# GpSimd waits for the end of its long instructions and adds the variance's epsilon in the attention half of a two-layer kernel

## The chip, the cores and the metric

One Trainium2 chip, one of its cores. A core has TensorE (PE, matrix products), VectorE (DVE), ScalarE (ACT), GpSimd (POOL) and SyncE (SP), which issues the DMAs here. Each engine runs its own instructions in order, and the engines meet at semaphores only. The metric is the device time of one execution in microseconds (us).

## The reference

Eight sequences of 1024 tokens with 256 channels go through attention in linear form (softmax over the 16 channels of a head for q, softmax over the tokens for k), a layer norm, an output projection, a residual and layer norm, and then a ternary feed-forward layer with its own residual and norm. The part around the change, all in f32:

```python
q = jax.nn.softmax(q, axis=-1)
k = jax.nn.softmax(k, axis=-2)
state = jnp.einsum('bhnd,bhne->bhde', k, v)
out = jnp.einsum('bhnd,bhde->bhne', q, state)
mu = out.mean(-1, keepdims=True)
var = out.var(-1, keepdims=True)
out = (out - mu) * jax.lax.rsqrt(var + EPS) * ln_g + ln_b
return out @ Wo.T + bo
...
x = _layernorm(x + attention(x))
```

## The kernel before

The program has two halves. The attention half takes the first 330 us, the feed-forward half the rest; the change touches the first only. Operands of the products are split into a rounded high part and the rest (`xt_hi`, `xt_lo`), and each product is made of three matmuls (high by high, low by high, high by low).

The attention half is a software pipeline. A loop of ten passes (b from 0 to 9) runs on every engine, and in pass b an engine does pieces of several sequences: the k product, the transposes and the state sum of sequence b, the q product and q denominator of sequence b+1, and the attention product, residual and norm of sequences b-1 and b-2. The order of the pieces within a pass is written out by hand for each engine. A sequence is eight token tiles of 128; g is 0 or 1 and names a group of four.

GpSimd's pass: `norm_rstd` of sequence b-2 (seven small instructions for each g), `q_normalise` twice (L299), `tok_lo` (L280, `xt_lo`), `q_denominator` of g=0 (L335, L337, L340, L343), `tok_lo`, `chan_lo` (L271, `xc_lo`), `tok_c` twice (L290, adds a row to the residual input), `attention_rstd` of g=0 (L308, `rsA` = `veA` to the power -1/2), `chan_lo`, `attention_rstd` of g=1, `q_denominator` of g=1. The instructions at L271, L280, L290 and L299 work on 1024 elements of each partition and have no wait of their own between them, except where an input comes from another engine.

VectorE's pass has, in the part that matters: `product_stats` (L684, `bnA`, the statistics of a tile of the attention product in PSUM `aps`), after tile 4 `out_variance` of g=0 (four aggregations L662 and then L664, `veA` = variance + EPS, for which GpSimd's L308 waits), then `product_stats` of tile 5 and the following, `out_variance` of g=1, `et_low`, then `residual` of g=0 (four instructions at L673, which read `z` and `xt`, and L678, `znm`), `sum_low` (L510, `xe_lo`), and `residual` of g=1.

ScalarE copies each tile of `aps` out (L411) after its statistics; TensorE may write the tile after next only then (L940). At the end of a pass TensorE finishes the state sum (L957), makes the first part of the next k product (L882), and then waits for `xe_lo` to make the state product (L896). After this come the q product and the transposes of the state (L907), ScalarE's `st_hi` (L417), its normalisation of the older sequence and, last, `xt_hi` (L380), which releases GpSimd's first `tok_lo` (L280) of the next pass. SyncE loads a sequence's `xt` and `xc` and stores the result ahead of need.

Of the kernel before, what the change touches and what calls it, by code (L numbers as in the profile page):

```python
# [27 lines left out]
ALU = mybir.AluOpType  # L28
# [4 lines left out]
EPS = 1e-5  # L33
# [14 lines left out]
def wait_for(eng, semaphore, count):  # L48

    if not isinstance(count, int) or count > 0:  # L50
        eng.wait_ge(semaphore, count)
# [24 lines left out]
def attention_phase(nc, kept, x_tok, x_chan, wq, wk, wv, wo, w1, w2, vecs_d, rows_d, ident_d, mask_d, x1_scratch):  # L76

    NB, _, T, C = x_tok.shape
    N = T * P
    CH = C // P  # L80
# [3 lines left out]
    GROUP = 4  # L84
    NG = T // GROUP
# [5 lines left out]
    with ExitStack() as ctx:  # L91
        def sb(name, shape, dt=F32):
            return ctx.enter_context(nc.sbuf_tensor(name, shape, dt))

        def sem(name):
            return ctx.enter_context(nc.semaphore(name))
# [48 lines left out]
        mvA = sb("mvA", [P, T, 2])  # L145
        veA = sb("veA", [P, T])
# [7 lines left out]
        eps = sb("eps", [P, T])  # L154
# [22 lines left out]
        xc_hi_ok, xc_lo_ok = sem("xc_hi_ok"), sem("xc_lo_ok")  # L177
        xt_hi_ok, xt_lo_ok, xt_c_ok = sem("xt_hi_ok"), sem("xt_lo_ok"), sem("xt_c_ok")
        k_mm, k_max, k_maxb, k_bias, k_exp = (sem(s) for s in ("k_mm", "k_max", "k_maxb", "k_bias", "k_exp"))
        q_mm, q_max, q_sub, q_exp = (sem(s) for s in ("q_mm", "q_max", "q_sub", "q_exp"))  # L180
        q_sum, q_inv, q_norm = (sem(s) for s in ("q_sum", "q_inv", "q_norm"))
# [7 lines left out]
        ap_mm, a_stat, a_var, a_eps, a_rstd = (sem(s) for s in ("ap_mm", "a_stat", "a_var", "a_eps", "a_rstd"))  # L189
# [72 lines left out]
        @block.gpsimd  # L262
        def _(pool):
            nc.gpsimd.memset(nhalf[:], -0.5).then_inc(half_ok, 1)

            def chan_lo(b, c):
                if not 1 <= b < NB:
                    return
                pool.wait_ge(xc_hi_ok, b + 1)
                wait_for(pool, k_mm, CH * (b - 1))  # L270
                nc.gpsimd.tensor_tensor(xc_lo[:, b % 2, c], xc[:, c], xc_hi[:, b % 2, c].bitcast(F32), ALU.subtract  # L271
                                        ).then_inc(xc_lo_ok, 1)

            def tok_lo(b, g):
                if not 0 <= b < NB:
                    return
                ts = slice(g * GROUP, (g + 1) * GROUP)
                pool.wait_ge(xt_hi_ok, b + 1)
                wait_for(pool, xe_mm, b)
                nc.gpsimd.tensor_tensor(xt_lo[:, ts], xt[:, b % 2, ts], xt_hi[:, ts].bitcast(F32), ALU.subtract  # L280
                                        ).then_inc(xt_lo_ok, 1)

            def tok_c(b, g):
                if not 0 <= b < NB:
                    return
                ts = slice(g * GROUP, (g + 1) * GROUP)
                pool.wait_ge(xt_lo_ok, NG * b + g + 1)
                if b == 0:
                    pool.wait_ge(rows_ok, 2)
                nc.gpsimd.tensor_tensor(xt[:, b % 2, ts], xt[:, b % 2, ts],  # L290
                                        c_row[:].rearrange("p (o c) -> p o c", o=1).to_broadcast([P, GROUP, C]),
                                        ALU.add).then_inc(xt_c_ok, 1)

            def q_normalise(b, g):
                if not 0 <= b < NB:
                    return
                pool.wait_ge(q_inv, NG * b + g + 1)
                v = qw[:, b % 2, g * GROUP:(g + 1) * GROUP].rearrange("p t (h d) -> p (t h) d", d=D)
                nc.gpsimd.tensor_tensor(  # L299
                    v, v, qinv[:, g].rearrange("p (h o) -> p h o", o=1).to_broadcast([P, GROUP * HEADS, D]),  # L300
                    ALU.mult).then_inc(q_norm, 1)

            def attention_rstd(b, g):
                if not 0 <= b < NB:
                    return
                gs = slice(g * GROUP, (g + 1) * GROUP)
                pool.wait_ge(a_eps, NG * b + g + 1)
                nc.gpsimd.tensor_tensor(rsA[:, gs], veA[:, gs], nhalf[:, gs], ALU.pow).then_inc(a_rstd, 1)  # L308

            def norm_rstd(b, g):  # L310
                if not 0 <= b < NB:
                    return
                gs = slice(g * GROUP, (g + 1) * GROUP)
                n = NG * b + g + 1
                pool.wait_ge(z_sq, T * b + GROUP * (g + 1))
                nc.gpsimd.tensor_tensor(vaZ[:, gs], zss[:, gs], inv_c[:, gs], ALU.mult).then_inc(z_var, 1)
                pool.wait_ge(z_var, n)
                nc.gpsimd.tensor_tensor(veZ[:, gs], vaZ[:, gs], eps[:, gs], ALU.add).then_inc(z_eps, 1)
                pool.wait_ge(z_eps, n)
                nc.gpsimd.tensor_tensor(rsZ[:, gs], veZ[:, gs], nhalf[:, gs], ALU.pow).then_inc(z_rstd, 1)  # L320
                pool.wait_ge(z_rstd, n)
                nc.gpsimd.tensor_tensor(nmr[:, gs], znm[:, gs], rsZ[:, gs], ALU.mult).then_inc(z_fin, 1)
                nc.gpsimd.tensor_tensor(vaZ[:, gs], vaZ[:, gs], rsZ[:, gs], ALU.mult).then_inc(z_fin, 1)
                pool.wait_ge(z_fin, 4 * n - 2)
                nc.gpsimd.tensor_tensor(vaZ[:, gs], vaZ[:, gs], rsZ[:, gs], ALU.mult).then_inc(z_fin, 1)
                pool.wait_ge(z_fin, 4 * n - 1)
                nc.gpsimd.tensor_tensor(z[:, gs, C], vaZ[:, gs], eps[:, gs], ALU.add).then_inc(z_fin, 1)

            def q_denominator(b, g):
                if not 1 <= b < NB:  # L330
                    return
                n = NG * (b - 1) + g
                pool.wait_ge(q_exp, NG * b + g + 1)
                v = qw[:, b % 2, g * GROUP:(g + 1) * GROUP].rearrange("p t (h d) -> p (t h) d", d=D)
                nc.gpsimd.tensor_tensor(qtree[:, g], v[:, :, 0:8], v[:, :, 8:16], ALU.add).then_inc(q_tree, 1)  # L335
                pool.wait_ge(q_tree, 3 * n + 1)
                nc.gpsimd.tensor_tensor(qtree[:, g, :, 0:4], qtree[:, g, :, 0:4], qtree[:, g, :, 4:8], ALU.add  # L337
                                        ).then_inc(q_tree, 1)
                pool.wait_ge(q_tree, 3 * n + 2)
                nc.gpsimd.tensor_tensor(qtree[:, g, :, 0:2], qtree[:, g, :, 0:2], qtree[:, g, :, 2:4], ALU.add  # L340
                                        ).then_inc(q_tree, 1)
                pool.wait_ge(q_tree, 3 * n + 3)
                nc.gpsimd.tensor_tensor(qsum[:, g], qtree[:, g, :, 0], qtree[:, g, :, 1], ALU.add).then_inc(q_sum, 1)  # L343

            nc.gpsimd.memset(inv_c[:], 1.0 / C).then_inc(half_ok, 1)
            nc.gpsimd.memset(eps[:], EPS).then_inc(half_ok, 1)
            pool.wait_ge(half_ok, 3)
            for c in range(CH):
                chan_lo(1, c)
            for b in range(NB + 2):  # L350
                norm_rstd(b - 2, 0)
                norm_rstd(b - 2, 1)
                q_normalise(b, 0)
                q_normalise(b, 1)
                tok_lo(b, 0)
                q_denominator(b + 1, 0)
                tok_lo(b, 1)
                chan_lo(b + 2, 0)
                tok_c(b, 0)
                tok_c(b, 1)  # L360
                attention_rstd(b - 1, 0)
                chan_lo(b + 2, 1)
                attention_rstd(b - 1, 1)
                q_denominator(b + 1, 1)
# [140 lines left out]
        def _(dve):  # L505
# [148 lines left out]
            def out_variance(b, g):  # L654
                if not 0 <= b < NB:
                    return
                ts = range(g * GROUP, (g + 1) * GROUP)
                gs = slice(g * GROUP, (g + 1) * GROUP)
                dve.wait_ge(a_stat, T * b + GROUP * (g + 1))
                nc.vector.memset(fence[:], 0.0)  # L660
                for t in ts:
                    nc.vector.bn_aggr(mvA[:, t], bnA[:, t]).then_inc(a_var, 1)  # L662
                dve.wait_ge(a_var, T * b + GROUP * (g + 1))
                nc.vector.tensor_scalar(veA[:, gs], mvA[:, gs, 1], EPS, None, ALU.add).then_inc(a_eps, 1)  # L664

            def residual(b, g):
                if not 0 <= b < NB:
# [78 lines left out]
            for b in range(NB + 2):  # L746
# [29 lines left out]
                pt_low(b, 0)  # L776
                product_stats(b - 1, 4)
                out_variance(b - 1, 0)
                product_stats(b - 1, 5)
                pt_low(b, 1)  # L780
# [816 lines left out]
```

## Time and profile before

| | us |
|---|---|
| median of 3 runs (637.6 to 639.22) | 637.66 |
| the profiled execution, its own time | 639.02 |
| span of the profile | 637.2 |
| attention half, about | 0 to 330 |
| GpSimd's first `tok_lo` of passes 1 to 6, starts | 70.1, 105.4, 143.7, 178.3, 214.5, 249.8 |

The profile shows for every instruction its start, its length and, where its engine was idle before it, which instruction of which engine released it. An engine name with nothing else is its work; "idle before" is the time in which it had none. Lines are those of the kernel before. Passes 1 to 5 are alike but for some preparation of the feed-forward weights on VectorE and ScalarE at the ends of passes 1 to 4.

### The profile page before, as it was taken

To read this page: it belongs to the slowest core of one execution; us is meant where nothing else is said; L and a number is where in the kernel's file an instruction comes from. 1 tells how busy PE (TensorE), PEld (TensorE's weight loads), DVE (VectorE), ACT (ScalarE), POOL (GpSimd) and SP (SyncE) were. 2 spreads that over 40 slices of the span, in tenths; PEclk is the share of its full clock that TensorE was granted. 3 is DMA by queue.
4 is the path that set the end of the run, shared out by engine and by line. 5 is a ranking of instruction groups with operands and counts; after the bars stand their busy time and mean duration, and the time that the engine had idled before them with its cause. 6 is when DMAs were issued, how large, how long until landed. Compare 5 with 4: busy or idle time off the path is not lost. (4 is left out here: it accounts for less than half of the span.)

```text
span 637.2 us, 10896 instructions
## 1 busy us (share of the span) xinstructions
PE 559.3 (88%) x3584; PEld 505.6 (79%) x3584; DVE 527.3 (83%) x1309; ACT 463.6 (73%) x906; POOL 427.5 (67%) x414
## 2 busy tenths in 40 slices
PE   1879999889998989979652999999999999999991
PEld 1769989879988979968551799888888888888890
DVE  3895798997979897868443479999999999999985
ACT  1253668476865848575554788999999999999983
POOL 0277887969988887783341556766767666776661
PEclk9899999989999999989685799999999999999996
DMA  7411004070402203030105100211112222200002
GB/s 269 168 67 67 1 6 194 1 264 2 163 36 91 109 2 133 1 132 2 66 8 225 33 34 2 62 55 53 53 46 67 68 67 67 68 34 33 34 34 99
DMA packets 10712, 46.53 MB, mean 73 GB/s; under 512 B 1312, under 2 KB 1568, under 8 KB 8352
## 3 DMA queue, kind: packets, MB, share of 16 engines
q1 hardware_dynamic: 10656, 45.83, 19.9%
q8 instruction: 29, 0.48, 0.3%
q14 instruction: 27, 0.22, 0.1%
HBM read 29.02 MB, written 16.81 MB: 72 GB/s over the span
## 5 line engine op out<-in xcount | busy, mean ns | idle before, releaser
L1518 PE MATMUL yps<-ff_w,ff_a_hi 128*128 128x258 f32 x512 | 125.8, 282 | 0.0
L1518 PE MATMUL yps<-ff_w,ff_a_lo 128*128 128x258 f32 x512 | 125.7, 282 | 0.0
L1502 PE MATMUL hps<-ff_ht_hi,t 128*128 128x512 f32 x256 | 107.5, 420 | 2.6 <-DVE ff_ht_lo L1301 2.6
L1309 DVE SCALAR_TENSOR_TENSOR ff_a_lo<-hps,ff_rho,ff_a_hi 128x512 fp32r<-128x512 f32 x128 | 91.6, 742 | 15.2 <-ACT ff_a_hi L1227 14.2
L1502 PE MATMUL hps<-ff_ht_lo,t 128*128 128x512 f32 x256 | 102.8, 402 | 0.0
L1518 PEld LDWEIGHTS yps<-ff_w,ff_a_hi 128*128 128x128 f32 x512 | 96.9, 189 | 3.4
L1518 PEld LDWEIGHTS yps<-ff_w,ff_a_lo 128*128 128x128 f32 x512 | 96.7, 189 | 3.3
L1213 ACT ACTIVATE hps<-hps,bias 128x512 f32<-128x512 f32 x128 | 83.9, 670 | 17.6 <-PE hps L1502 16.2
L1185 POOL TENSOR_TENSOR ff_accp<-ff_accp,ff_sq 128x512 f32<-128x512 f32 x64 | 83.9, 1311 | 10.6 <-ACT ff_sq L1225 5.9
L1225 ACT ACTIVATE ff_sq<-hps 128x512 f32<-128x512 f32 x128 | 78.4, 612 | 0.6
L1227 ACT CAST ff_a_hi<-hps 128x512 fp32r<-128x512 f32 x128 | 77.3, 604 | 0.0
L1172 POOL TENSOR_TENSOR ff_x1c<-ff_x,ff_c_row 128x512 f32<-128x512 f32 x32 | 37.4, 1191 | 48.5 <-DVE ff_z L1370 48.5
L1502 PEld LDWEIGHTS hps<-ff_ht_hi,t 128*128 128x128 f32 x256 | 49.1, 192 | 17.9 <-DVE ff_ht_lo L1301 5.5
L940 PE MATMUL aps<-r_hi,pt_hi 128*128 128x384 f32 x128 | 48.2, 376 | 11.8 <-DVE r_lo L510 6.7
L1502 PEld LDWEIGHTS hps<-ff_ht_lo,t 128*128 128x128 f32 x256 | 49.4, 193 | 7.6
L411 ACT COPY z<-aps 128x256 f32<-128x256 f32 x64 | 23.4, 382 | 38.2 <-DVE bnA L684 38.0
L280 POOL TENSOR_TENSOR xt_lo_then_t<-xt,xt_hi 128x1024 fp32r<-128x1024 f32 x16 | 39.4, 2462 | 16.9 <-ACT xt_hi L380 16.9
L684 DVE BATCH_NORM_STATS2 bnA<-aps 128x6 f32<-128x256 f32 x64 | 26.8, 427 | 27.1 <-PE aps L940 27.0
L271 POOL TENSOR_TENSOR xc_lo<-xc,xc_hi 128x1024 fp32r<-128x1024 f32 x14 | 33.5, 2396 | 19.1 <-ACT xc_hi L373 19.1
L940 PE MATMUL aps<-r_lo,pt_hi 128*128 128x384 f32 x128 | 44.5, 347 | 0.0
L940 PE MATMUL aps<-r_hi,pt_lo 128*128 128x384 f32 x128 | 44.3, 346 | 0.0
L1370 DVE SCALAR_TENSOR_TENSOR ff_z<-ff_yc,ff_gain,ff_x1c 128x256 f32<-128x256 f32 x64 | 41.6, 691 | 0.0
(186 smaller groups left out, 1716.8 us busy)
## 6 DMA issues: line engine op xcount, KB each, us to landing
x_scratch<-z SPq DMA_DIRECT2D x16, 514.0 KB, 2.8
ff_x<-x_scratch SPq DMA_DIRECT2D x16, 514.0 KB, 4.9
xc<-in_x_chan_dram SPq DMA_DIRECT2D x8, 1024.0 KB, 6.8
xt<-in_x_tok_dram SPq DMA_DIRECT2D x8, 1024.0 KB, 4.8
out_dram<-ff_z SPq DMA_DIRECT2D x16, 512.0 KB, 3.4
w_raw<-in_w_dram SPq DMA_DIRECT2D x2, 1024.0 KB, 4.8
rows<-in_rows_dram SPq DMA_DIRECT2D x1, 512.0 KB, 4.2
w_raw<-in_wq_dram SPq DMA_DIRECT2D x1, 256.0 KB, 2.6
```

The source lines that it names most:

```text
L271: nc.gpsimd.tensor_tensor(xc_lo[:, b % 2, c], xc[:, c], xc_hi[:, b % 2, c].bitcast(F32), ALU.subtract).then_inc(xc_lo_ok, 1)
L280: nc.gpsimd.tensor_tensor(xt_lo[:, ts], xt[:, b % 2, ts], xt_hi[:, ts].bitcast(F32), ALU.subtract).then_inc(xt_lo_ok, 1)
L940: last = nc.tensor.matmul(out, l, r, start=(c == 0 and k == 0), stop=(c == CH - 1 and k == 2), skip_group_check=True)
L1172: nc.gpsimd.tensor_tensor(x1c[:, k % 2, ts], x1[:, k % XB, ts, 0:C], c_row[:].rearrange("p (o c) -> p o c", o=1).to_broadcast([P, n, C]), ...
L1185: nc.gpsimd.tensor_tensor(accp[:], a, sq[:, m], ALU.add).then_inc(sum_p, 1)
L1213: nc.scalar.activation(ring(k, m), ring(k, m), ACT.Gelu, bias=bias1[:, m:m + 1]).then_inc(gelu_ok, 1)
L1225: nc.scalar.activation(sq[:, m], ring(k, m), ACT.Square).then_inc(sq_ok, 1)
L1227: nc.scalar.copy(a_hi[:, m % DEPTH], ring(k, m)).then_inc(hi_ok, 1)
L1309: nc.vector.scalar_tensor_tensor(out=a_lo[:, m % DEPTH], in0=ring(k, m), scalar=rho[:, m:m + 1], in1=a_hi[:, m % DEPTH].bitcast(F32), op0= ...
L1370: nc.vector.scalar_tensor_tensor(out=z[:, k % 2, t], in0=yc[:, t], scalar=gain[:, t:t + 1], in1=x1c[:, k % 2, t], op0=ALU.mult, op1=ALU.ad ...
L1502: mm = nc.tensor.matmul(ring(k, m), t1[:, c, m * P:(m + 1) * P], h[:, k % 2, c], start=(c == 0 and j == 0), stop=(c == CH - 1 and j == 1))
L1518: last = nc.tensor.matmul(yps[:, t, 0:C + 2], a[:, m % DEPTH, t * P:(t + 1) * P], w2[:, m], start=(m == 0 and j == 0), stop=(m == FC - 1 a ...
```

## The change

In the attention half GpSimd gets a wait for the semaphore of its own instruction after each `chan_lo`, `tok_lo`, `tok_c` and `q_normalise`, 62 in all, so that its next instruction starts only when the long one has ended. VectorE no longer adds EPS to the variance: L664 and the wait ahead of it go away (16 times), and GpSimd waits for the aggregations (`a_var`) and makes `veA` itself, from `mvA` and the constant tile `eps`, right before the power. The order of all other instructions is kept.

```diff
 def chan_lo(b, c):
...
                 nc.gpsimd.tensor_tensor(xc_lo[:, b % 2, c], xc[:, c], xc_hi[:, b % 2, c].bitcast(F32), ALU.subtract
                                         ).then_inc(xc_lo_ok, 1)
+                pool.wait_ge(xc_lo_ok, CH * b + c + 1)
...
                 nc.gpsimd.tensor_tensor(xt_lo[:, ts], xt[:, b % 2, ts], xt_hi[:, ts].bitcast(F32), ALU.subtract
                                         ).then_inc(xt_lo_ok, 1)
+                pool.wait_ge(xt_lo_ok, NG * b + g + 1)
...
                                         ALU.add).then_inc(xt_c_ok, 1)
+                pool.wait_ge(xt_c_ok, NG * b + g + 1)
...
                     ALU.mult).then_inc(q_norm, 1)
+                pool.wait_ge(q_norm, NG * b + g + 1)
...
 def attention_rstd(b, g):
...
                 gs = slice(g * GROUP, (g + 1) * GROUP)
+                pool.wait_ge(a_var, T * b + GROUP * (g + 1))
+                nc.gpsimd.tensor_tensor(veA[:, gs], mvA[:, gs, 1], eps[:, gs], ALU.add).then_inc(a_eps, 1)
                 pool.wait_ge(a_eps, NG * b + g + 1)
                 nc.gpsimd.tensor_tensor(rsA[:, gs], veA[:, gs], nhalf[:, gs], ALU.pow).then_inc(a_rstd, 1)
...
                     nc.vector.bn_aggr(mvA[:, t], bnA[:, t]).then_inc(a_var, 1)
-                dve.wait_ge(a_var, T * b + GROUP * (g + 1))
-                nc.vector.tensor_scalar(veA[:, gs], mvA[:, gs, 1], EPS, None, ALU.add).then_inc(a_eps, 1)
```

GpSimd in a steady pass, from the second `tok_lo` to the second denominator, before (names are output and inputs; in brackets the semaphores that the instruction waits for):

```order
L280 TENSOR_TENSOR xt_lo_then_t<-xt,xt_hi 128x1024 [waits xe_mm,xt_hi_ok]
L271 TENSOR_TENSOR xc_lo<-xc,xc_hi 128x1024 [waits k_mm,xc_hi_ok]
L290 TENSOR_TENSOR xt<-xt,c_row 128x1024 [waits xt_lo_ok] x2
L308 TENSOR_TENSOR rsA<-veA,nhalf 128x4 [waits a_eps]
L271 TENSOR_TENSOR xc_lo<-xc,xc_hi 128x1024 [waits k_mm,xc_hi_ok]
L308 TENSOR_TENSOR rsA<-veA,nhalf 128x4 [waits a_eps]
L335 TENSOR_TENSOR qtree<-qw 128x512 [waits q_exp]
```

and the same piece after the change:

```order
L281 TENSOR_TENSOR xt_lo_then_t<-xt,xt_hi 128x1024 [waits xe_mm,xt_hi_ok]
L271 TENSOR_TENSOR xc_lo<-xc,xc_hi 128x1024 [waits k_mm,xc_hi_ok,xt_lo_ok]
L292 TENSOR_TENSOR xt<-xt,c_row 128x1024 [waits xt_lo_ok,xc_lo_ok]
L292 TENSOR_TENSOR xt<-xt,c_row 128x1024 [waits xt_lo_ok,xt_c_ok]
L312 TENSOR_TENSOR veA<-mvA,eps 128x4 [waits a_var,xt_c_ok]
L314 TENSOR_TENSOR rsA<-veA,nhalf 128x4 [waits a_eps]
L271 TENSOR_TENSOR xc_lo<-xc,xc_hi 128x1024 [waits k_mm,xc_hi_ok]
L312 TENSOR_TENSOR veA<-mvA,eps 128x4 [waits a_var,xc_lo_ok]
L314 TENSOR_TENSOR rsA<-veA,nhalf 128x4 [waits a_eps]
L341 TENSOR_TENSOR qtree<-qw 128x512 [waits q_exp]
```

Each instruction behind a long one has got that one's semaphore, and `veA` stands ahead of each power. Behind the power there is no new wait. The denominator of g=0, ahead of this piece, waits for the first `tok_lo` in the same way.

VectorE around the variance of g=0, before:

```order
L662 BN_AGGR mvA<-bnA 128x2 x4
L664 TENSOR_SCALAR veA<-mvA 128x4 [waits a_var]
L684 BN_STATS bnA<-aps 128x6 [waits ap_mm]
L510 TENSOR_TENSOR pt_lo<-ring,pt_hi 128x512 [waits pt_hi_ok]
L510 TENSOR_TENSOR et_lo<-ring,et_hi 128x512 [waits et_hi_ok]
```

and after:

```order
L668 BN_AGGR mvA<-bnA 128x2 x4
L688 BN_STATS bnA<-aps 128x6 [waits ap_mm]
L516 TENSOR_TENSOR pt_lo<-ring,pt_hi 128x512 [waits pt_hi_ok]
L516 TENSOR_TENSOR et_lo<-ring,et_hi 128x512 [waits et_hi_ok]
```

The statistics of tile 5 follow the aggregations directly.

## Rows read from the trace of the kernel before

**Rows 1.** First section of the page: busy time and share of the span
```profile
PE 559.3 (88%) x3584; PEld 505.6 (79%) x3584; DVE 527.3 (83%) x1309; ACT 463.6 (73%) x906; POOL 427.5 (67%) x414
```

**Rows 2.** Waits, 20 to 300 us: waiter, awaited, total us, times, longest
```profile
PE aps L940 <- ACT z L411: 5.0, 6, 1.1
...
PE sps L896 <- DVE xe_lo L510: 3.5, 4, 1.0
```

**Rows 3.** Groups on VectorE, 0 to 330 us: busy us, mean ns, idle before
```profile
L664 DVE TENSOR_SCALAR veA<-mvA 128x4 f32<-128x4 f32 x16 | 14.9, 929 | 0.5
```

**Rows 4.** Order of time on GpSimd: start us, length us, engine, line, operation
```profile
163.06 1.52 POOL L335 TENSOR_TENSOR qtree<-qw 128x512 f32<-128x512 f32 x1
...
178.25 2.46 POOL L280 TENSOR_TENSOR xt_lo_then_t<-xt,xt_hi 128x1024 fp32r<-128x1024 f32 x1 [2.45 <-ACT xt_hi L380]
180.67 1.27 POOL L335 TENSOR_TENSOR qtree<-qw 128x512 f32<-128x512 f32 x1
182.02 0.73 POOL L337 TENSOR_TENSOR qtree<-qtree 128x256 f32<-128x256 f32 x1
...
192.99 1.03 POOL L308 TENSOR_TENSOR rsA<-veA,nhalf 128x4 f32<-128x4 f32 x1
193.98 2.42 POOL L271 TENSOR_TENSOR xc_lo<-xc,xc_hi 128x1024 fp32r<-128x1024 f32 x1
196.33 1.25 POOL L308 TENSOR_TENSOR rsA<-veA,nhalf 128x4 f32<-128x4 f32 x1
197.56 1.28 POOL L335 TENSOR_TENSOR qtree<-qw 128x512 f32<-128x512 f32 x1
...
202.21 0.20 POOL L318 TENSOR_TENSOR veZ<-vaZ,eps 128x4 f32<-128x4 f32 x1
```

**Rows 5.** Order of time on VectorE, 185 to 200 us
```profile
185.94 2.45 DVE L664 TENSOR_SCALAR veA<-mvA 128x4 f32<-128x4 f32 x1
...
195.39 1.33 DVE L673 SCALAR_TENSOR_TENSOR z<-z,rsA,xt 128x256 f32<-128x256 f32 x1
...
196.65 0.48 DVE L673 SCALAR_TENSOR_TENSOR z<-z,rsA,xt 128x256 f32<-128x256 f32 x1
...
197.46 1.66 DVE L673 SCALAR_TENSOR_TENSOR z<-z,rsA,xt 128x256 f32<-128x256 f32 x1
...
199.16 0.57 DVE L678 TENSOR_SCALAR znm<-zsum 128x4 f32<-128x4 f32 x1
199.65 0.68 DVE L510 TENSOR_TENSOR xe_lo<-sps,xe_hi 128x512 fp32r<-128x512 f32 x1
```

**Rows 6.** Order of time on TensorE, 165 to 201 us; idle before in brackets
```profile
165.25 0.39 PE L896 MATMUL sps<-w_hi,xe_hi 128*128 128x256 f32 x1
...
189.19 0.44 PE L940 MATMUL aps<-r_hi,pt_hi 128*128 128x384 f32 x1 [1.08 <-ACT z L411]
...
200.38 0.39 PE L896 MATMUL sps<-w_hi,xe_hi 128*128 128x256 f32 x1 [0.96 <-DVE xe_lo L510]
```

**Rows 7.** Order of time on ScalarE, 170 to 179 us
```profile
170.23 0.37 ACT L417 CAST st_hi<-sps 128x256 fp32r<-128x256 f32 x1 [0.83 <-PE sps L907]
...
176.27 1.91 ACT L380 CAST xt_hi<-xt 128x2048 fp32r<-128x2048 f32 x1
```

**Rows 8.** TensorE: an idle time; windows: length, busy, granted clock, DMA share, GB/s
```profile
134.26 0.44 PE L907 MATMUL sps<-ident,r_f 128*128 128x128 f32 x2 [2.01 <-DVE r_f L622]
...
133.90:137.40 3.50, 3.14 (x17) 0.73 0.86 311
137.40:140.80 3.40, 3.40 (x16) 0.77 1.01 356
200.40:203.80 3.40, 3.40 (x22) 1.00 0.25 39
```

**Rows 9.** Order of time on VectorE in the first pass, 39 to 43 us
```profile
39.15 2.31 DVE L604 TENSOR_TENSOR kbm<-kmx,vecs 128x1 f32<-128x1 f32 x1
41.50 1.19 DVE L607 TENSOR_TENSOR kbias<-vecs,kbm 128x1 f32<-128x1 f32 x1
```

## The prediction

> **What bounds the kernel now.** I read the share of the engines first, then who TensorE waits for, and then the order of time in one steady pass of the attention half, engine by engine. TensorE is the busiest engine [rows 1]. In the attention half it waits 5.0 us in six places for ScalarE's copy of the attention product, and 3.5 us in four places for `xe_lo` of VectorE [rows 2]. The first wait comes from VectorE: L664, an addition on four elements, takes 2.45 us in a steady pass [rows 5] and 929 ns on average [rows 3]. It starts at 185.94 and ends at 188.39, together with GpSimd's `chan_lo`; the same happens to L673 at 195.39, which ends 0.32 us after `chan_lo` (193.98 to 196.40) [rows 4, 5]. So some VectorE instructions can't run while GpSimd runs a long one.
>
> The second wait is the one that sets the period. State product to state product is 200.38 - 165.25 = 35.13 us [rows 6], and it can be followed as one chain without a hole: state product 165.25 to `st_hi` 170.23, ScalarE busy from there to `xt_hi` at 176.27 [rows 7], GpSimd's first `tok_lo` at 178.25, GpSimd never idle until the second `chan_lo` ends at 196.40 [rows 4], VectorE's four L673, `znm` and `xe_lo` at 199.65 [rows 5], and TensorE, idle for 0.96 us, at 200.38 [rows 6]. TensorE's own work is shorter: 35.13 less the waits of 1.08 and 0.96 is about 33.1 us. The bound of a steady pass is thus GpSimd's row of instructions together with VectorE's hold-ups behind it, and TensorE has 2.0 us to spare.
>
> **Part 1, L664 leaves VectorE.** Sixteen instructions with 14.9 us [rows 3] go; at 0.17 us each, undisturbed, 2.7 of these would be work and 12 are the hold-up. VectorE is ahead by 2.3 us at tile 5, and TensorE's wait of 1.08 us in the pass goes. But neither lies on the chain above: L673 starts only when GpSimd has made `rsA` and lets go at the end of the second `chan_lo`. The gain becomes a longer idle time of TensorE ahead of the state product. On the path this part is worth 0.
>
> **Part 2, the waits on GpSimd.** Without a wait the next instruction starts 0.04 us before the end of the one ahead (192.99 + 1.03 = 194.02, next at 193.98); with one it starts 0.08 us behind it (180.67 + 1.27 = 181.94, next at 182.02) [rows 4]. A wait costs 0.12 to 0.13 us. On the chain from 178.25 to the end of the second `chan_lo` lie five: behind both `tok_lo`, the first `chan_lo` and both `tok_c`. That is 0.65 us. The two behind `q_normalise` are covered by GpSimd's idle time of 2.45 us ahead of `tok_lo` [rows 4].
>
> **Part 3, the addition on GpSimd.** A four-element addition takes 0.20 us [rows 4] and the power waits 0.08 for it: 0.28 us per group. The one of g=0 stands on the chain. The second `chan_lo` ends 0.65 + 0.28 = 0.93 us later, counted from `xt_hi`. It is queued directly behind `rsA`, starts before VectorE hears of `rsA`, and holds L673 off to its end as before. [...]
>
> **Part 4, what VectorE meets behind `chan_lo`.** Call the end of the second `chan_lo` E. Before: the first L673 ends at E + 0.32, the others follow at 0.41 intervals, and the last starts at E + 1.06 (197.46). GpSimd's L335 starts at 197.56, 0.10 later by the record, and yet the L673 takes 1.66 instead of 0.48: it loses [rows 4, 5]. Then `znm` loses some more to L337, and `xe_lo` starts at E + 3.25. In pass 3 L335 took 1.52 instead of 1.28 [rows 4], so there VectorE won: it is a race within hundredths. After: `veA` is asked for at E + 0.08, is held by the first L673 until about E + 0.17 (the power behind `chan_lo`, 1.25 instead of 1.03, shows 0.2 of such a delay [rows 4]), the power starts near E + 0.46, is held once more for 0.1, and ends near E + 1.60. L335 comes at E + 1.56. The last L673 is past by then (0.5 us ahead; it wins). `znm` is asked for at E + 1.58: it loses, and is let go at L335's end, E + 1.56 + 1.28 = E + 2.84; `xe_lo`, which starts 0.08 us before the end of `znm`, comes at E + 2.78. That is 0.47 us earlier than before, against 0.93 later for E: **+0.46 us per pass**. The bounds are `znm` winning (`xe_lo` at E + 1.67: -1.58 + 0.93 = -0.65) and the last L673 losing again (about +1.3). I take the middle case, since `znm` would need to be asked for 0.1 us ahead of L335 and is about level with it.
>
> Passes 1, 2, 4 and 5: 4 x 0.46 = 1.8. Pass 3, where VectorE won before: L335 starts at E + 1.16 (197.56 - 196.40), holds `znm` alone for its 1.52, and `xe_lo` came at 1.16 + 1.52 - 0.08 = E + 2.60. From there to E + 2.78 is 0.18 later, and with 0.93 it is 1.1. Passes 6 to 8 have no `chan_lo` and wait for other engines; I take +0.4 from two waits and two additions that get into the path (the last pass has no cover for them).
>
> **Part 5, the start.** In pass 0 `kbm` (L604) takes 2.31 us and L607 1.19 [rows 9], since GpSimd's `tok_lo` had started just before L604 and its L335 came ahead of L607. The two waits behind `q_normalise` start that `tok_lo` 0.26 later, about level with L604. If L604 wins, L607 is held to the end of `tok_lo` only, near 41.46 + 0.26 = 41.7 in place of 42.69, 0.95 us earlier than now; if not, all is 0.4 later. I take -0.4.
>
> Sum without the clock: 1.8 + 1.1 + 0.4 - 0.4 = **+2.9 us**.
>
> **Part 6, TensorE's clock.** [...] With the change the two waits of a pass, 2.04 us in two pieces, become one of 2.04 + 0.46 = 2.5 us, right before the product that starts the chain. [...]
>
> **The sum**: +2.9 + 2.5 = +5.4 us. Against the profiled execution that is 639.02 + 5.4 = 644.4. That execution is 1.4 us above the median; from the median, 637.66 + 5.4 = **643.1 us**.
>
> **The rivals.**
> A, `znm` wins the race against L335. For it: L335's place is worked out to 0.1 us only, and each more hold on GpSimd helps `znm`. Then 4 x -0.65 = -2.6, pass 3 -0.93 + 0.93 = 0, rest 0: 635.0. TensorE's idle time is 1.4 us, and the clock stays. It decides from 0.1 us between `znm` and L335.
> B, TensorE is the bound after all, and every wait for the copies that goes shortens the kernel: -5.0, 632.7. [...] The trace speaks against it: the chain through GpSimd has no hole, and TensorE waits for its end in every pass but one.
> C, the clock does not fall, or only where it is covered: 640.6.
> D, the last L673 is still held, by `veA` pushing it back: 5 x 1.3 = 6.5 and a clock loss of 5: 649.
> E, the waits cost nothing, since GpSimd's early starts are records and no overlap: per pass 0.28 - 0.47 = -0.2, sum about -1; or races fall differently from pass to pass and cancel: 636 to 639.
>
> **How the numbers follow.** About 0.3% (1.9 us) is what a measurement of this kernel can tell from no change. Forecast with some clock loss 0.39, C 0.17, D 0.06: slower 0.62. E 0.13: same. A 0.17, B 0.08: faster 0.25. The range leaves out B and D and what lies past them: 634.5 to 647.5. The slower cases alone reach from 639.6 to 649.
>
> **What would show it.** In the profile after: GpSimd's starts 0.12 later behind each long instruction; 18.15 us from `tok_lo` to E become 19.1; L664's time gone and no TensorE wait for the copies in passes 1 to 6; the last L673 0.48 long and `znm` about 1.3 long; one idle time of TensorE of about 2.5 us ahead of each state product; the period 35.6 us or more. A period of 34.5 and a `znm` of 0.17 would be A; a period near 33.5 would be B, and my chain would be wrong. A granted clock of 1.00 behind the long idle times would take part 6 away.

## The result, and the profile after

The changed kernel takes 642.72 us, median of 5 runs (641.17 to 644.77), against 637.6 us before (635.71 to 639.22, 5 runs). The ratio is 1.0092, with a 95% interval of 1.0057 to 1.0127. The profiled execution took 644.52 us with a span of 642.4 us, 5.2 us more than before. Lines below are those of the changed kernel; L677 is the residual (L673 before), L682 is `znm` (L678), L341 the denominator (L335), L516 `xe_lo` (L510), L900 the state product (L896).

Who TensorE waited for, from 20 to 300 us (waiter, awaited: total us, times, longest):

```profile
PE sps L900 <- DVE xe_lo L516: 12.4, 5, 2.8
...
PE aps L944 <- DVE r_lo L516: 2.4, 1, 2.4
```

The wait for ScalarE's copies, 5.0 us in six places before, is gone, and the wait for `xe_lo` went from 3.5 us to 12.4 [rows 2]. The wait for `r_lo` is not new: before, it was 2.25 us, ahead of 280.81. GpSimd in the pass that answers to [rows 4] (start, length):

```profile
179.09 2.44 POOL L281 TENSOR_TENSOR xt_lo_then_t<-xt,xt_hi 128x1024 fp32r<-128x1024 f32 x1 [3.20 <-issue]
181.61 1.27 POOL L341 TENSOR_TENSOR qtree<-qw 128x512 f32<-128x512 f32 x1
...
194.43 0.20 POOL L312 TENSOR_TENSOR veA<-mvA,eps 128x4 f32<-128x4 f32 x1
194.71 1.02 POOL L314 TENSOR_TENSOR rsA<-veA,nhalf 128x4 f32<-128x4 f32 x1
195.70 2.40 POOL L271 TENSOR_TENSOR xc_lo<-xc,xc_hi 128x1024 fp32r<-128x1024 f32 x1
198.17 0.26 POOL L312 TENSOR_TENSOR veA<-mvA,eps 128x4 f32<-128x4 f32 x1
198.51 1.14 POOL L314 TENSOR_TENSOR rsA<-veA,nhalf 128x4 f32<-128x4 f32 x1
199.62 1.25 POOL L341 TENSOR_TENSOR qtree<-qw 128x512 f32<-128x512 f32 x1
```

From the first `tok_lo` to the end of the second `chan_lo`, E, it is 198.10 - 179.09 = 19.01 us, against 18.15 before. VectorE behind E = 198.10, to be held against [rows 5]:

```profile
195.76 2.62 DVE L677 SCALAR_TENSOR_TENSOR z<-z,rsA,xt 128x256 f32<-128x256 f32 x1 [0.90 <-POOL rsA L314]
...
199.12 0.48 DVE L677 SCALAR_TENSOR_TENSOR z<-z,rsA,xt 128x256 f32<-128x256 f32 x1
...
199.64 1.26 DVE L682 TENSOR_SCALAR znm<-zsum 128x4 f32<-128x4 f32 x1
200.81 0.68 DVE L516 TENSOR_TENSOR xe_lo<-sps,xe_hi 128x512 fp32r<-128x512 f32 x1
```

The last of the four residual instructions is free (0.48 in place of 1.66), `znm` is held for the length of L341 (1.26 in place of 0.57), and `xe_lo` starts at E + 2.71. TensorE in the same pass, and its granted clock (windows: length, busy, clock, DMA share, GB/s):

```profile
201.54 0.39 PE L900 MATMUL sps<-w_hi,xe_hi 128*128 128x256 f32 x1 [2.74 <-DVE xe_lo L516]
...
126.50:130.30 3.80, 3.78 (x16) 0.55 0.23 39
130.30:133.70 3.40, 2.80 (x20) 1.00 0.86 299
201.50:205.00 3.50, 3.46 (x15) 0.56 0.23 33
```

Two idle times became one of 2.7 us, and in the 3.5 us behind it the granted clock was 0.56 on average.

### The profile page after: what moved, and what is told of

Its sections match the earlier page's. It is cut to its first block and busy times, and to the rows that moved or that the text cites. A ratio compares the mean times of both kernels' runs of the same rounds, so it can differ in the third digit from the quotient of the medians.

```text
span 642.4 us, 10941 instructions
## 1 busy us (share of the span) xinstructions
PE 561.3 (87%) x3584; PEld 509.0 (79%) x3584; DVE 522.7 (81%) x1293; ACT 463.8 (72%) x906; POOL 433.1 (67%) x430
## 5 line engine op out<-in xcount | busy, mean ns | idle before, releaser
L1313 DVE SCALAR_TENSOR_TENSOR ff_a_lo<-hps,ff_rho,ff_a_hi 128x512 fp32r<-128x512 f32 x128 | 91.6, 743 | 13.5 <-ACT ff_a_hi L1231 12.4
L453 ACT ACTIVATE zjunk<-z,znm 128x256 f32<-128x256 f32 x64 | 31.8, 498 | 20.1 <-DVE znm L682 20.1
L677 DVE SCALAR_TENSOR_TENSOR z<-z,rsA,xt 128x256 f32<-128x256 f32 x64 | 40.6, 689 | 4.1 <-POOL rsA L314 4.1
```

The lines of the kernel that those rows point to most:

```text
L677: nc.vector.scalar_tensor_tensor(out=z[:, t, 0:C], in0=z[:, t, 0:C], scalar=rsA[:, t:t + 1], in1=xt[:, b % 2, t], op0=ALU.mult, op1=ALU.ad ...
L1313: nc.vector.scalar_tensor_tensor(out=a_lo[:, m % DEPTH], in0=ring(k, m), scalar=rho[:, m:m + 1], in1=a_hi[:, m % DEPTH].bitcast(F32), op0= ...
```

## The experiments

A state product starts each pass for TensorE, so the distance between two of them is the length of a pass, and it repeats within 0.15 us between two traces of the changed kernel but for the last one, 7->8. The two traces of the kernel before differ more, which is taken up under the repeats. Every trace is of one execution. This table, from the starts of L896 or its like in each profile, is what the verdicts rest on most; the medians of whole runs scatter more.

```
distance to the next state product, us:
pass              1->2   2->3   3->4   4->5   5->6   6->7   7->8   sum, 1 to 7
                        (state products 1 to 8)
before            34.60  35.14  37.72  35.13  36.35  32.66  32.20  211.6
before again      40.80  34.35  37.09  34.45  35.79  32.66  32.22  215.1
changed           34.94  35.53  38.08  36.94  37.11  34.30  33.21  216.9
changed again     34.96  35.56  38.08  37.08  37.06  34.36  31.92  217.1
epsilon alone     34.39  34.87  37.50  34.90  36.46  32.69  30.42  210.8
waits alone       34.56  35.10  37.68  35.09  36.43  32.64  30.52  211.5
znm first         33.86  34.85  38.11  34.79  36.89  32.76  30.78  211.3
k twice           35.03  35.56  38.90  35.56  36.89  33.88  29.73  215.8
```

The column 2->3 is free of a fall of the clock on the path in all of them (1.00 from one product to the next); "sum" is the first six columns. 2->3 and 4->5 are the passes whose period was 35.13 in the prediction.

**Epsilon alone, and the waits alone.** From the changed kernel, the four kinds of wait behind long instructions are taken out (first), or the addition is put back on VectorE (second).

```diff
-                pool.wait_ge(xc_lo_ok, CH * b + c + 1)
...
-                pool.wait_ge(xt_lo_ok, NG * b + g + 1)
...
-                pool.wait_ge(xt_c_ok, NG * b + g + 1)
...
-                pool.wait_ge(q_norm, NG * b + g + 1)
```

> The addition of epsilon on GpSimd alone, no waits behind the long instructions. Chain theory: the second chan_lo of a pass ends 0.28 us later, the last L673 escapes the denominator and znm is held by it, so xe_lo comes 0.47 - 0.28 = 0.2 us earlier per pass; TensorE's idle time gathers into one of about 1.85 us, with or without a fall of the clock. Together -1 us, or up to +2 with falls: ratio 0.998 to 1.003. Rival, TensorE is the bound: -5 us, ratio 0.992. Rival, the addition on GpSimd is what costs: +4 us or more, ratio 1.006.

```diff
-                pool.wait_ge(a_var, T * b + GROUP * (g + 1))
-                nc.gpsimd.tensor_tensor(veA[:, gs], mvA[:, gs, 1], eps[:, gs], ALU.add).then_inc(a_eps, 1)
...
+                dve.wait_ge(a_var, T * b + GROUP * (g + 1))
+                nc.vector.tensor_scalar(veA[:, gs], mvA[:, gs, 1], EPS, None, ALU.add).then_inc(a_eps, 1)
```

> The waits behind the long instructions alone, epsilon stays on VectorE. Chain theory: five waits of 0.13 us lie on the chain, 0.65 us per pass in five passes, the last L673 is still held by the denominator, and TensorE's two idle times stay two, of 1.1 and 1.6 us, with no fall of the clock: +3.3 us, ratio 1.005. Rival, all of GpSimd's time counts: 62 x 0.13 = +8 us, ratio 1.013. Rival, waits are free: ratio 1.000.

Epsilon alone: 1.0009 (0.9985 to 1.0032), the pass 2->3 0.27 us shorter (34.87 against 35.14). The chain theory holds with its -0.2. Waits alone: 1.0011 (0.9992 to 1.0029), where 1.005 was expected, and passes as long as before (35.10). VectorE and, below it, GpSimd in pass 2 of the waits alone show where the cost was made good:

```profile
122.00 2.54 DVE L677 SCALAR_TENSOR_TENSOR z<-z,rsA,xt 128x256 f32<-128x256 f32 x1
...
125.28 0.47 DVE L677 SCALAR_TENSOR_TENSOR z<-z,rsA,xt 128x256 f32<-128x256 f32 x1
125.80 1.10 DVE L682 TENSOR_SCALAR znm<-zsum 128x4 f32<-128x4 f32 x1
126.81 0.68 DVE L514 TENSOR_TENSOR xe_lo<-sps,xe_hi 128x512 fp32r<-128x512 f32 x1
```

```profile
121.87 2.39 POOL L271 TENSOR_TENSOR xc_lo<-xc,xc_hi 128x1024 fp32r<-128x1024 f32 x1
124.33 1.07 POOL L312 TENSOR_TENSOR rsA<-veA,nhalf 128x4 f32<-128x4 f32 x1
125.38 1.50 POOL L339 TENSOR_TENSOR qtree<-qw 128x512 f32<-128x512 f32 x1
```

E is 124.26. The last residual instruction wins: it is 0.47 long, and it is now the denominator that takes 1.50 in place of 1.28. `xe_lo` starts at E + 2.55 in place of E + 3.25, 0.7 us earlier, and this pays for the five waits. I had taken the race to be lost there. It is not shown that the wait behind `chan_lo` decides it: by the record the denominator starts 0.10 us behind the last residual instruction here (125.28, 125.38), as it does in [rows 4, 5], where the race was lost. The race was won in passes 1 to 5 of this trace.

Each part alone is thus worth nothing, or a little less, and together they are worth +5.3 in the sum of the table (216.9 against 211.6, the first trace of the kernel before). The pass whose first `tok_lo` starts at 177 to 179 us (pass 4) shows why the halves don't add up. From the first `tok_lo` to E it is 18.15 us before, 18.44 with epsilon alone, 18.74 with the waits alone and 19.01 with both, so these costs add. From E to `xe_lo` it is 3.25 before, and 2.72, 2.56 and 2.71: the last residual instruction gets out of the denominator's way in each of the three, and this gain of 0.5 to 0.7 us can be had only once. The clock comes on top: with both, TensorE's idle times ahead of the third to sixth state product are 2.2 to 2.8 us and the clock fell behind all four (0.54 to 0.62 as the mean of the 3.5 us behind); with epsilon alone they are 1.6 to 2.1, and it fell within 1.5 us behind two of them (0.72 and 0.61); with the waits alone they are 1.1 to 1.5, and it fell behind none (1.00).

**`znm` first.** The second denominator of a pass waits for `znm` of the pass, in the changed kernel.

```diff
 def q_denominator(b, g):
...
                 pool.wait_ge(q_exp, NG * b + g + 1)
+                if g == 1 and b >= 2:
+                    pool.wait_ge(z_mean, NG * (b - 2) + 1)
```

> The changed kernel, with GpSimd's second denominator of a pass waiting for znm of the residual, so that znm can't lose the race. Chain theory: znm takes 0.17 us in place of 1.26, xe_lo comes 1.1 us earlier per pass, TensorE's idle time falls from 2.7 to about 1.6 us and the clock stays up: 5 to 6 us from znm and 3 from the clock below the changed kernel, 634 us against 642.7, ratio to the kernel before 0.995. Without an effect of the clock 637, ratio 1.000. Rival, the race is not on the path and only the waits are: 642.7, ratio 1.008.

The ratio is 1.0023 (1.0003 to 1.0043): below the changed kernel, but not below the one before. VectorE and TensorE in pass 2:

```profile
123.28 0.17 DVE L684 TENSOR_SCALAR znm<-zsum 128x4 f32<-128x4 f32 x1
123.36 0.68 DVE L518 TENSOR_TENSOR xe_lo<-sps,xe_hi 128x512 fp32r<-128x512 f32 x1
123.96 1.19 DVE L679 SCALAR_TENSOR_TENSOR z<-z,rsA,xt 128x256 f32<-128x256 f32 x1
...
125.08 0.94 DVE L679 SCALAR_TENSOR_TENSOR z<-z,rsA,xt 128x256 f32<-128x256 f32 x1
```

```profile
132.07 0.44 PE L913 MATMUL sps<-ident,r_f 128*128 128x128 f32 x2 [3.25 <-DVE r_f L630]
```

`znm` takes 0.17 and `xe_lo` comes at E + 1.6, as expected, but the denominator now holds the second residual (1.19 and 0.94 in place of 0.5), and in pass 3->4, where weights are prepared, TensorE waits 3.25 us for VectorE's `r_f` ahead of the transposes, in place of 0.60 in the changed kernel. Of 1.1 us per pass 0.7 stay (34.85 against 35.53), and in pass 3->4 nothing. So the race is on the path, but the 634 us that I expected were missed (median 638.44), since the hold-up in part changes place. No fall of the clock is seen in passes 1 to 6 (1.00 throughout), where the idle times ahead of the state products are 0.8 to 1.7 us.

**The k product made twice.** Six matmuls of 1.56 us are repeated ahead of the state product, in the changed kernel, and change no result.

```diff
                 k_product(b, 0, 0)
+                if 2 <= b < NB:
+                    k_product(b, 0, 0)
                 state_product(b - 1)
```

> The changed kernel, in passes 2 to 7 with the first half of the first k product (six matmuls, 1.56 us) made twice, in the idle time ahead of the state product, which comes out the same. Clock theory: the idle time falls from 2.7 to 1.1 us, no clock falls behind it in passes 2 to 5, and the passes 4, 5 and 6 are 1 to 1.6 us shorter: -3.5 us against the changed kernel, ratio to the kernel before 1.003. Rival, the falling clock costs nothing on the path: as the changed kernel, 1.008, or more by what doesn't fit in (passes 6 and 7 have little idle time, +1.5 us each).

The ratio is 1.0013 (0.9982 to 1.0044), with more work on TensorE than the changed kernel has. TensorE at the fourth state product, which starts the pass 4->5, and the clock behind it, first in this kernel:

```profile
163.14 0.39 PE L900 MATMUL sps<-w_hi,xe_hi 128*128 128x256 f32 x1 [0.45 <-DVE xe_lo L516]
...
163.10:166.60 3.50, 3.46 (x22) 1.00 0.13 23
```

and in the changed kernel:

```profile
164.60 0.58 PE L900 MATMUL sps<-w_hi,xe_hi 128*128 128x256 f32 x1 [2.23 <-DVE xe_lo L516]
...
164.60:168.10 3.50, 3.50 (x15) 0.54 0.17 26
```

The idle time is 0.45 us in place of 2.23, the clock stays at 1.00, and the pass goes from 36.94 to 35.56 us, which is the length of pass 2->3 in both kernels. The clock costs 1.4 us in a pass where nothing else hides it. This is the clearest single result: in this pass VectorE and GpSimd do the same in both kernels, with `znm` held for 1.27 and 1.26 us. The gain is smaller elsewhere. The idle times ahead of the third, fifth and sixth state products are 1.32, 1.33 and 1.32 us in place of 2.71, 2.74 and 2.79, and the clock is 1.00 in the 3.5 us behind each, where it was 0.55, 0.56 and 0.62: that much of the clock theory is shown. Passes 5->6 and 6->7, which have the repeated matmuls too, are 0.2 and 0.4 us shorter. Pass 3->4 is 0.8 us longer: the clock stayed at 1.00 behind its state product, but fell behind 131.11, after 2.13 us of waiting for `r_f` (0.60 as the mean of 131.1 to 135.3).

**Variants of the kernel before.** One wait alone, behind the second `chan_lo`:

```diff
                                         ).then_inc(xc_lo_ok, 1)
+                if c == 1:
+                    pool.wait_ge(xc_lo_ok, CH * b + c + 1)
```

> The kernel before with one wait per pass, behind the second chan_lo, none behind the other long instructions. Race theory: E does not move, the power and the denominator behind it come 0.1 us later, and that is enough for the last L673 to get in ahead of the denominator (0.48 in place of 1.66 us); znm is held in its place, xe_lo comes at about E + 2.6 in place of E + 3.25, and passes 1, 2, 4 and 5 are up to 0.65 us shorter: -2.6 us, ratio 0.996. Rival, the waits-only kernel gained its 0.65 by the epsilon addition getting in ahead of a chan_lo: here L664 is held for 2.4 us as before, and the ratio is 1.000 or a little more.

1.0031 (0.9986 to 1.0075), and inconclusive. Its passes 2->3 to 5->6 are 34.38, 37.09, 34.47 and 35.84 us, 0.5 to 0.8 shorter than in the first trace of the kernel before, as expected. But the kernel before again shows the same numbers without the wait (34.35, 37.09, 34.45, 35.79). So the wait isn't shown to do anything.

The denominator waiting for `znm`, in the kernel before (the diff as above):

> The kernel before, with GpSimd's second denominator of a pass waiting for znm. Chain theory: xe_lo at E + 1.6 in place of E + 3.25 with E where it was; the second residual then meets the denominator and gives back 0.4 to 1 us; the period goes from 35.13 to about 34.2 us, where TensorE's own work with its wait of 1.1 us is the bound: -3 to -4 us, ratio 0.995. Rival, hold-ups of VectorE only change places: ratio 1.000.

1.0002 (0.9964 to 1.0041). The passes 2->3 to 5->6 take 34.08, 36.69, 34.62 and 35.42 us, 3.5 us less together than in the first trace of the kernel before, but 1->2 takes 40.80, 6.2 us more: L666, the epsilon addition there, was held for 6.72 us. The second trace of the kernel before has this long pass too (40.80), and beside it the four passes are only 0.9 us less together.

```profile
74.66 6.72 DVE L666 TENSOR_SCALAR veA<-mvA 128x4 f32<-128x4 f32 x1
```

The same with two waits more, behind the first `chan_lo` and the first `tok_c`:

```diff
+                if c == 0:
+                    pool.wait_ge(xc_lo_ok, CH * b + c + 1)
...
+                if g == 0:
+                    pool.wait_ge(xt_c_ok, NG * b + g + 1)
```

> The kernel before with the denominator waiting for znm, as in the run before, and waits behind the first chan_lo and the first tok_c. Gap theory: where GpSimd's long instructions follow without a gap, a VectorE instruction can be passed over at the boundary; with the 0.08 us gap it gets in at the first one. So L664 of pass 1 takes at most 2.5 us in place of 6.72, no TensorE wait of 5.4 us in pass 1, against 0.26 us per pass for the waits: ratio 0.996. Rival, the 6.72 us come from something else than the missing gap (a transfer, the phase of the pass) and stay: ratio 1.001 or more.

0.9968 (0.9941 to 0.9995), median 636.15, passes 1->2 to 5->6 33.91, 34.07, 38.53, 34.04 and 35.82 us. In pass 1 the addition took:

```profile
77.51 2.10 DVE L670 TENSOR_SCALAR veA<-mvA 128x4 f32<-128x4 f32 x1
```

GpSimd's `tok_c` starts 0.07 us behind the end of `chan_lo` there (77.20 + 2.39 = 79.59, next at 79.66), and the addition got in at that boundary, at 79.61. In the run before, without the two waits, it starts 0.03 us before that end (74.38 + 2.38 = 76.76, next at 76.73), and the addition was passed over there. That is what the gap theory expects, but one trace each isn't proof, since the kernel before shows both (2.08 in the first trace, 6.73 in the second). There is a rival: in the three traces with the long hold the addition starts 0.28 to 0.29 us behind `chan_lo`, and in this one and the first trace of the kernel before 0.31 and 0.32, so a small shift of the start may decide as well. Pass 7 is a better comparison. There the addition of g=0 was asked for 1.3 to 1.8 us after the first of two `tok_c` had started, without the waits (`znm` first in the kernel before) and with them (waits alone):

```profile
287.15 2.94 DVE L666 TENSOR_SCALAR veA<-mvA 128x4 f32<-128x4 f32 x1
```

```profile
287.88 0.78 DVE L668 TENSOR_SCALAR veA<-mvA 128x4 f32<-128x4 f32 x1
```

Without a wait behind the first `tok_c` it was held to the end of the second, here and in the kernel before with both halves of the k product ahead ("k ahead", the runs below; 3.14 us); with the wait it got in at the end of the first, here and with k ahead on the waits alone (1.15 us). That is two traces against two, for the gap theory.

Both halves of the k product ahead of the state product, in the kernel before, in the changed kernel and in the waits alone:

```diff
                 k_product(b, 0, 0)
-                state_product(b - 1)
                 k_product(b, 0, 1)
+                state_product(b - 1)
```

> The kernel before, with both halves of the first k product ahead of the state product. Chain theory: TensorE is idle for 0.96 us there, so the state product comes 0.6 us later, but the 1.56 us of the second half no longer stand between it and the transposes of the state: 0.96 us per pass shorter in passes 1, 2, 4 and 5, with TensorE the bound then: -3.5 us, ratio 0.994. Rival, TensorE's order doesn't matter since VectorE's s_f and r_f are what the transposes wait for: ratio 1.000, and a new wait ahead of the transposes in the profile.

> The changed kernel with both halves of the first k product ahead of the state product. Chain theory: 1.56 us of TensorE's idle 2.7 us are filled, the state product comes when it did, the transposes 1.56 us earlier if VectorE's r_f allows, and the clock stays up: 1 to 1.5 us per pass and 4 us of clock below the changed kernel, ratio to the kernel before 0.996 to 0.999. Rival, r_f is what the transposes wait for: only the clock is gained, 1.002.

> The waits behind the long instructions, epsilon left on VectorE, and both halves of the first k product ahead of the state product. Chain theory: in the waits-only kernel TensorE is idle for 1.5 us ahead of the state product, and this is now filled with work that stood on the chain: up to 1.5 us less in passes 1, 2, 4 and 5, none of L664 held: -4 to -5 us, ratio 0.993. Rival, VectorE's r_f holds the transposes as it did in the passes that prepare weights: 0.996, no better than k ahead without the waits.

In the kernel before: 0.9963 (0.9927 to 0.9998), median 638.07 against 639.14; passes 1->2, 2->3 and 4->5 are 33.77, 33.72 and 33.58 us long, 0.8 to 1.5 shorter than in the first trace. In the changed kernel: 1.0022 (0.9989 to 1.0054), where the rival had 1.002. On the waits alone: 1.0003 (0.9969 to 1.0037), though its passes are among the shortest (33.83, 34.25, 37.83, 34.29, 36.49); its trace is of a run of 635.98 us, one of the shortest of 12 with a median of 640.17. Both theories are right in part. In pass 3->4, with the most preparation, TensorE of the kernel before with k ahead now waits longer for `r_f`,

```profile
132.33 0.44 PE L907 MATMUL sps<-ident,r_f 128*128 128x128 f32 x2 [3.52 <-DVE r_f L622]
```

and the pass is only 0.4 us shorter. Passes 5->6 and 6->7 are 1.1 and 1.3 us longer (37.49 and 33.95): TensorE waits 2.29 and 1.27 us for `r_f` there, and the clock fell behind the first (0.54 as the mean of 202.0 to 205.5). Two versions came out 0.3 to 0.4% below the kernel before, k ahead and `znm` first with two waits, each with the end of its interval close to 1. The repeat of the kernel before, which follows, is as far from 1, so neither is shown to be faster than it.

**Both kernels once more.**

> The changed kernel once more, beside these runs, for a second trace of it. All theories: ratio 1.009 (1.006 to 1.013); in the trace the first L673 held for 2.6 us, znm for 1.26 in each of passes 1 to 5, no VectorE instruction held over a boundary of two GpSimd instructions, and the clock falling behind the idle times of more than 2 us ahead of the state product, though perhaps not behind each.

> The kernel before once more, for a second trace of it: ratio 1.000, which shows what the comparison can tell. If being passed over is chance, this trace may show an L664 of 4.8 or 6.7 us somewhere, or none as in the first; the periods of passes 2 and 4 stay at 35.1 us unless a race behind the second chan_lo falls the other way, which makes one 34.5.

The changed kernel again: 1.0068 (1.0039 to 1.0097), median 643.47 of 12 runs. The kernel before again: 1.0040 (1.0001 to 1.0079), though it is the same kernel; its 12 runs lie from 637.1 to 646.0 and those of the changed kernel from 641.7 to 644.7. A difference below about 0.4% from one such comparison is therefore not to be trusted, and the lengths of passes say more. The medians of the two repeats are 2.0 us apart (643.47 and 641.47), and so are their sums in the table (217.1 and 215.1). Against the 35 other runs of the kernel before, with a median of 638.18, the changed kernel is 5.3 us longer. So the price of the change lies between 2 and 5 us, by the way in which the kernel before ran. What spreads the kernel before is seen in its second trace. VectorE in pass 1, GpSimd beside it, and TensorE behind it:

```profile
74.93 6.73 DVE L664 TENSOR_SCALAR veA<-mvA 128x4 f32<-128x4 f32 x1
```

```profile
74.64 2.40 POOL L271 TENSOR_TENSOR xc_lo<-xc,xc_hi 128x1024 fp32r<-128x1024 f32 x1
76.99 4.64 POOL L290 TENSOR_TENSOR xt<-xt,c_row 128x1024 f32<-128x1024 f32 x2
```

```profile
82.45 0.69 PE L940 MATMUL aps<-r_hi,pt_hi 128*128 128x384 f32 x1 [5.38 <-ACT z L411]
```

L664 was held over three GpSimd instructions to 81.66, and TensorE stood for 5.38 us. In its passes 2 to 5 the last residual instruction won its race, 0.1 us ahead of the denominator by the record, where it had lost with the same distance in four of five passes of the first trace:

```profile
127.28 0.48 DVE L673 SCALAR_TENSOR_TENSOR z<-z,rsA,xt 128x256 f32<-128x256 f32 x1
```

```profile
127.38 1.53 POOL L335 TENSOR_TENSOR qtree<-qw 128x512 f32<-128x512 f32 x1
```

So the kernel before has several ways to run: all passes of middle length, or one long and four short ones. The second way cost 3.5 us more up to the seventh state product and had begun 3.35 us earlier, so both traces have the eighth at the same time (301.59 and 301.78). The long pass came in the three traces with L664 on VectorE and no wait behind the first `chan_lo` whose first state product lay at 54.2 to 56.5 us, and not in the two at 57.8 and 58.0; whether the start decides is open. The changed kernel has one way, seen twice.

## Why the prediction was right

**The time.** 643.1 was forecast, 642.72 measured, inside 634.5 to 647.5 and on the forecast side. The chain, the race and the fall of the clock came as described; that the sum came so close is luck, as Part 6 shows.

**Part 1** holds: L664 and TensorE's waits for the copies went, and the pass did not become shorter; the gain turned into idle time ahead of the state product (0.96 to 2.74 us).

**Parts 2 and 3** hold: 19.01 against 18.15 us is +0.86, where 0.93 was forecast. The waits cost 0.12 each, and the addition and its gap 0.28 (194.43 to 194.71). The +0.4 that was taken for passes 6 to 8 is not seen where the clock stays: pass 6->7 is 32.69 and 32.64 with either half, against 32.66.

**Part 4** holds in its likeliest case: L341 starts at E + 1.52 (E + 1.56 forecast), `znm` at E + 1.54 (1.58) and loses, `xe_lo` starts at E + 2.71 (2.78). The pass without a clock effect is 35.53 against 35.14: +0.39 for +0.46. That the waits alone cost nothing is consistent with this sum but not with what I expected of that experiment: there the race of the last residual instruction decides, and I had it on the wrong side. Pass 3->4 was mis-sized: +0.36 in place of +1.1. In the kernel before, the fall of the clock behind 134.26 lay on this pass's path. Its second trace has the same race won in this pass and no fall of the clock (1.00 from 134 to 146), and the pass is 37.09 in place of 37.72: the fall cost 0.6 us. In the changed kernel the clock fell earlier, behind 126.52, and the wait ahead of the transposes shrank from 2.01 us:

```profile
133.37 0.44 PE L911 MATMUL sps<-ident,r_f 128*128 128x128 f32 x2 [0.60 <-DVE r_f L628]
```

So the 0.6 us that the kernel before had paid are no longer paid there, which makes up most of the difference. That is worked out from traces, with no run made for it.

**Part 5** has its first step right. `kbm` won its race against `tok_lo`, and `kbias` (L613, L607 before) was held once, to 41.83 in place of 42.69 [rows 9]:

```profile
39.21 0.16 DVE L610 TENSOR_TENSOR kbm<-kmx,vecs 128x1 f32<-128x1 f32 x1
39.41 2.42 DVE L613 TENSOR_TENSOR kbias<-vecs,kbm 128x1 f32<-128x1 f32 x1
```

This is so in all seven traces with waits behind `q_normalise` and in none of the seven without: counted from the start of the reduction ahead of `kbm`, `kbias` ends 3.9 us later with them and 4.8 to 4.9 without. What of these 0.9 us reaches the first state product is not shown: it came at 56.06 against 57.78, but the second traces have it at 54.10 and 54.43, for the changed kernel and the one before, so most of the 1.7 us is the scatter of the start.

**Part 6** was mis-sized. No run shows the 2.5 us for the clock in the sum, nor the clock loss of 5 us in rival D. By an estimate from [rows 8], where the clock is 0.73 and 0.77 over 3.5 and 3.4 us, one fall takes up to 1.7 us. What the runs showed for all of them is more than the 2.5 and less than the 5: 1.4 in pass 4->5 (36.94 against 35.53), 0.4 in 5->6, 1.6 in 6->7 (34.30 against 32.66) and 1.0 in 7->8, 4.4 together. The last did not come again: the second trace of the changed kernel has 31.92 in 7->8, against 32.20 before. The chain gave 1.9 instead of 2.9 (0.34 + 0.39 + 0.36 + 0.39 + 0.39). With -1.7 at the start that is 1.9 + 4.4 - 1.7 = 4.6, the difference of the last state product (306.16 - 301.59 = 4.57), and 0.6 us came after it. So the sum was hit by errors that cancel: the chain was taken 1.0 us too high, the start 1.3 and passes 6 to 8 0.4, the clock 1.9 too low, and no part had the 0.6 us at the end.

**The rivals.** A (`znm` wins) didn't happen in either trace, and the run that forced it shows that it would have brought 0.7 us per pass rather than 1.1, since the denominator then holds the next residual. B (TensorE is the bound) is out: its waits for the copies went and the kernel became slower. TensorE is the busiest engine (87% of the span), and 5.0 us of its waits were removed, but a chain through the other engines set the period. C (no fall of the clock) is out: the clock was 0.54 to 0.62 over the 3.5 us behind the idle times ahead of the third to sixth state products. D (the last residual instruction is still held) is out too: it takes 0.48 us. E's statement that waits cost nothing is right for the waits alone, by another mechanism: each does cost 0.12 us, and a won race gives it back.

## What to carry to other kernels

A gain on one engine is worth what the chain that sets the period lets through. Two gaps of the busiest engine, of 1.08 and 0.96 us, became one of 2.74 here, and that cost the clock on top (0.56 in place of 1.00 over the next 3.5 us). VectorE's last residual instruction started 0.10 us ahead of GpSimd's denominator in both traces of the kernel before, and took 1.66 us in one (197.46) and 0.48 in the other (127.28): a race that either may win, and 0.5 to 0.7 us per pass hung on it. Two halves that each cost nothing cost 5 us together, since both lived on winning the same race: costs add up, and a race is won only once. If a kernel's runs spread by 1%, take a second trace of it before explaining a difference.

## What the runs showed of the hardware

A VectorE instruction on four elements (L664) was held for 6.72 to 6.73 us, over three GpSimd instructions in a row, in the second trace of the kernel before and in two variants of it (one wait alone, `znm` first); like ones took 2.94 and 3.14 us over one boundary. L664 waits for `a_var` alone, which VectorE raises itself, so these two engines meet not only at semaphores. A single GpSimd instruction held it to its end: L664 at 78.29, asked for 0.32 us into a `chan_lo`, ended at 80.37, where the `chan_lo` ended at 80.35. At the end of a GpSimd instruction it was not always the longer waiting engine that went next: in the second trace of the kernel before L664 had waited from 74.93, and GpSimd's `tok_c` went at 76.99. All the cases in which VectorE was passed over had GpSimd instructions that followed without a gap (the next one starts 0.03 to 0.05 us before the end of the one ahead); with a gap of 0.08 us between them none was seen held over a boundary in the 14 traces.

The clock fell behind idle times of TensorE of 2.2 to 2.8 us in the changed kernel's passes 2 to 5, in both traces, to 0.53 to 0.63 as the mean of the 3.5 to 4.6 us behind. Within such a fall it is 0.50: from 126.9 to 130.2 in the changed kernel, and from 135.6 to 138.9 in the kernel before [rows 8]. It didn't fall behind the 1.9 us of the changed kernel's pass 1, nor behind 1.3 to 1.7 us ahead of state products in the variants (1.00 over 3.5 us). But of the idle times of 2.05, 2.08 and 2.13 us in epsilon alone two had a fall behind them, and behind the 3.25 us of the run with `znm` first and the 3.52 and 3.53 us of two with k ahead it stayed up (1.00 over 3.5 us), while behind the 3.53 us of the third it was 0.68. The length of one idle time alone doesn't tell it, and what does stays open.
